# Idle products on TensorE in the tail of a convolution and attention kernel

## The reference

```
x = x + L0(_gn(x))     # _gn: group norm, 32 groups of 8 channels, per image
x = x + L1(_gn(x))
```

```
sim = jnp.where(mask, neg, sim)      # mask is true on real pixels
attn = jax.nn.softmax(sim, axis=-1)
out = jnp.einsum('bij,bjd->bid', attn, v)
out = out @ Wout_w.T + Wout_b
```

## Time and profile before

| | |
|---|---|
| device time of the three runs, median | 225.84 us |
| device time of the profiled execution | 225.6 us |
| its span, first to last instruction | 223.8 us |
| outside the span | 1.8 us |
| PE busy | 188.3 us (84% of the span) |
| DVE, ACT, POOL busy | 138.9, 134.8, 91.6 us |
| mean granted TensorE clock over the span | 0.98 |

### The profile page before, as it was taken

The page is one execution under the profiler, slowest core; times in us unless marked ns, Lnnn a source line. Parts: engine busy times, 40 slices in busy tenths (PEclk is TensorE's granted clock), DMA queues, the critical chain, the costliest instruction groups (busy, mean ns, idle before and its releaser), DMA issues.

```text
span 223.8 us, 3513 instructions
## 1 busy us (share of the span) xinstructions
PE 188.3 (84%) x1116; PEld 69.0 (31%) x1116; DVE 138.9 (62%) x338; ACT 134.8 (60%) x228; POOL 91.6 (41%) x203
## 2 busy tenths in 40 slices
PE   0003999799999999999999999999999999999440
PEld 0003243325323323233342333334333244334130
DVE  0487768956025866546665855867558675587932
ACT  0395779891324685909566595683955857559710
POOL 2005050524722513132396742359475139904331
PEclk9999999999999999999999999999999999999965
DMA  6999999995835769546867899799798898992705
GB/s 213 411 410 410 408 409 409 405 265 127 226 95 156 196 194 267 157 116 187 261 183 256 234 294 295 221 303 272 219 294 260 281 271 260 319 351 98 254 27 187
DMA packets 30802, 57.06 MB, mean 255 GB/s; under 512 B 3264, under 2 KB 12224, under 8 KB 30784
## 3 DMA queue, kind: packets, MB, share of 16 engines
q1 hardware_dynamic: 30400, 56.55, 78.8%
q10 hardware_dynamic: 384, 0.29, 0.4%
HBM read 17.85 MB, written 16.78 MB: 155 GB/s over the span
## 4 chain that ended last, share of the span: by engine, by line
PE 73%; DMA 9%; SPq 6%; DVE 4%; POOL 3%; ACT 2%; issue 1%; DVEq 0%; ACTq 0%; POOLq 0%
PE py L818 37%; PE pf L849 25%; DMA xs<-x_dram 9%; SPq L262 6%; PE pf L764 3%; PE py L866 3%; PE py L764 2%; DVE gs L560 2%; ACT junk L529 2%; POOL gs L353 1%; PE pf L778 1%; DVE xs L254 1%; POOL chain L400 0%; POOL chain L438 0%; POOL y L363 0%
## 5 line engine op out<-in xcount | busy, mean ns | idle before, releaser
L818 PE MATMUL py<-gs,wd 80*32 80x512 f32 x768 | 86.1, 594 | 0.0
L529 ACT ACTIVATE junk<-xs,nwb 128x1024 bf16<-128x1024 f32 x63 | 72.3, 1148 | 4.0 <-DVE xs L655 1.5
L655 DVE SCALAR_TENSOR_TENSOR xs<-pf,cst,xs 128x512 f32<-128x512 f32 x64 | 48.1, 751 | 21.0 <-PE pf L849 16.0
L849 PE MATMUL pf<-y,fw 128*128 128x512 f32 x128 | 59.1, 604 | 0.0
L509 ACT ACTIVATE y<-py,cst 128x512 f32<-128x512 f32 x32 | 20.3, 684 | 54.5 <-PE pf L849 49.6
L381 POOL TENSOR_TENSOR wd<-vals,cst 80x384 f32<-80x384 f32 x30 | 25.2, 844 | 56.2 <-PE py L818 55.9
L664 DVE SCALAR_TENSOR_TENSOR y<-py,cst,y 128x512 f32<-128x512 f32 x32 | 22.6, 747 | 35.1 <-PE py L818 35.0
L818 PEld LDWEIGHTS py<-gs,wd 80*32 80x32 f32 x768 | 23.1, 109 | 57.2 <-issue 56.5
L849 PEld LDWEIGHTS pf<-y,fw 128*128 128x128 f32 x128 | 23.0, 190 | 33.0 <-issue 33.0
L560 DVE BATCH_NORM_STATS2 gs<-xs 128x6 f32<-128x512 f32 x40 | 25.0, 681 | 12.0 <-DMA xs<-x_dram 11.9
L458 ACT ACTIVATE wd<-xs 128x1024 bf16<-128x1024 f32 x24 | 25.0, 1044 | 4.2 <-DMA xs<-x_dram 4.2
(11 more groups left out here) (84 smaller groups left out, 88.6 us busy)
## 6 DMA issues: line engine op xcount, KB each, us to landing
gs<-fc SPq DMA_DIRECT2D x128, 169.4 KB, 3.0
xs<-x_dram SPq DMA_DIRECT2D x15, 1024.0 KB, 18.8
out_dram<-xs SPq DMA_DIRECT2D x32, 256.0 KB, 3.1
out_dram<-xs SPq DMA_DIRECT2D x16, 512.0 KB, 3.9
xs<-x_dram SPq DMA_DIRECT2D x2, 512.0 KB, 17.3
gs<-wkv_dram SPq DMA_DIRECT2D x1, 256.0 KB, 15.5
gs<-wout_t_dram SPq DMA_DIRECT2D x1, 256.0 KB, 15.5
fw<-fusion_dram SPq DMA_DIRECT2D x1, 256.0 KB, 10.5
```

The source lines that it names most:

```text
L529: act.activation(junk[:, :], x1(n, c), func, scale=scale, bias=bias[:, c:c + 1], accum_out=acc[:, n, c, e:e + 1]).then_inc(s_stat, 1)
L655: dve.scalar_tensor_tensor(out=rows[:, t], in0=image(pf[:, bank * HALF:(bank + 1) * HALF]), scalar=fb[:, c:c + 1], in1=rows[:, t], op0=ALU ...
L818: mm = pe.matmul(py[n % 2][quad(q), s * HALF:(s + 1) * HALF], wd[0:KP, w0:w0 + QUAD], rows, start=(j == 0), stop=(j == PASSES - 1))
L849: pe.matmul(pf[:, bank * HALF:(bank + 1) * HALF], fw[:, t * C + 128 * c:t * C + 128 * (c + 1)], y[:, t * HALF:(t + 1) * HALF], start=True, ...
```

## The change

PE issues a product six times whose result nothing reads. Each is a float32 product of 128 x 512, of the shape of a fusion product, with its operands in place (`fw`, `y`) and its output in `py[0][:, 0:HALF]`, the bank that `attention(EARLY)` wrote. Four stand behind the last fusion and ahead of the last group product, two stand between the last group product and the last attention product. One wait is added ahead of the four: for `s_vec` at EARLY + 1, which DVE sets when it has copied the result of `attention(EARLY)` out of that bank. The products set no semaphore and wait for nothing else.

```diff
--- before
+++ after
@@ -911,8 +911,15 @@
                     f_late(3)
             pe.wait_ge(s_vec, EARLY)
             attention(EARLY)
+            def idle_products(count):
+                for _ in range(count):
+                    pe.matmul(py[0][:, 0:HALF], fw[:, 0:128], y[:, 0:HALF], start=True, stop=True)
+
             fuse(N - 1)
+            pe.wait_ge(s_vec, EARLY + 1)
+            idle_products(4)
             group_product(FINAL)
+            idle_products(2)
             attention(FINAL)
```

## The result

Over 20 executions of each kernel the changed one takes 225.31 us in the median (224.41 to 228.38), the kernel before 226.99 us (225.49 to 229.33). The ratio is 0.9948 with a 95% interval of 0.9926 to 0.9970: about 0.5% less, 1.2 us, and within the 1% that was called no change. The profiled execution takes 224.59 us at a span of 222.7 us (before: 225.6 and 223.8). Without that the means of the 20 give 0.9961 and the two medians 0.9926; why the medians jump is shown further down.

What follows compares the result with a forecast made beforehand. The prediction took the tail's chain of waits, with PE mostly idle and its clock falling before the last attention product, as the bound. Terms 0 + 0 + 0 + 0 - 0.85 us took 225.84 to 225.0 us, range 224.4 to 226.3.

Steps and rivals of the forecast that it cites:

- The term of the clock: Last attention product: clock stays at 1.00, so it takes 1.03 in place of 1.88 us, saving 0.85 us.
- The cost of the products: Idle products around the last group product: 0.43 us a record, hidden in PE's idle time, cost 0.
- The added wait: Behind the last fusion: the early result's copy is done some 3 us before PE waits for it, cost 0.
- DVE and ACT beside a busy PE: Tail residuals and statistics: not slowed by the idle products, bounded at 0 to 0.05 us, taken as 0.
- The reach to the end: Behind the last attention product: copy, adds and last stores follow it, so the whole 0.85 us reaches the end.
- The weight loads: Last attention product: eight loads follow the clock, 0.97 us high and 1.78 us low, against the skill's clock-independent rule.
- The rival of the overrun: Between last group and attention products: two idle products at low clock overrun their cover, 1.4 us late, 227.2 us; chance 0.05.
- The base of the sum: Whole kernel: level before taken as 225.84 us, the median of the runs, from which 0.85 us was subtracted.

Runs made afterwards that it cites:

- only the first fills: Kernel before plus four idle products (256, 512, 256, 384 columns) in PE's first-stage gaps, with nothing added in the tail; ratio 0.9970 (0.9940 to 0.9999).
- the pair alone: Changed kernel without the four products ahead of the last group product, keeping the two behind it; ratio to the kernel before 1.0013 (0.9980 to 1.0045).
- the second set: The unaltered changed kernel run once more against the kernel before, 12 executions; median 226.23 us, ratio 0.9948 (0.9910 to 0.9986).
- four and four: Changed kernel with four instead of two products between the last group and attention products; ratio to the kernel before 1.0003 (0.9966 to 1.0040).
- four only: Changed kernel without the two products behind the last group product, run twice; ratios to the kernel before 0.9956 first, 0.9970 second.

## Why the prediction was right

- *The time.* 225.0 us was forecast and 225.31 us measured, in the stated range of 224.4 to 226.3. Within 1% was right.
- *The term of the clock.* 0.85 us was forecast from the two attention products of before. The profile has 0.82 (1.88 to 1.06) for the product and 0.83 for the chain up to its end. Group by group over all executions (89 and 32), the mean span of the lowest group goes from 223.87 to 222.83 us and that of the next from 225.45 to 224.41, 1.04 us each. The ratio says 1.2 us, with an interval of 0.7 to 1.7 us on 227. I had written that nothing in the rows could be shortened beyond 0.85, since the group product ran at 1.00. That step was too narrow: the run with only the first fills shows a fall ahead of the group product, 0.2 us more to save, and the mean clocks say that the clock was low for longer than in the first profile in 26 of the 37 lowest executions of before.
- *The cost of the products.* 0.43 us a record and ends 0.4 and 0.2 us ahead of what follows were forecast; the distance is 0.43 (weight loads as before), the gaps left are 0.43 and 0.20 us. With two products more at either place the delay was 1.12 and 1.35 us, against an arithmetic of 1.1 to 1.3 and 1.3 to 1.5.
- *The added wait.* It cost nothing: the idle products begin at 209.10, 0.17 us ahead of the end of the fusion's last record (205.59 + 3.68), as a next record of the fusion would, since its records overlap by about as much (0.59 us long, 0.43 apart).
- *DVE and ACT beside a busy PE.* The tail's residuals stayed at 752 ns and the statistics at 1148 ns, as the rows said.
- *The reach to the end.* The last stores are issued from 218.2 (forecast 218.35), the span is 222.7 (forecast 222.95), 0.2 us of it from ahead of the tail.
- *The weight loads.* The rule of the page "TensorE: Matmul & The Clock Gate" of the Trainium skill, section "LDWEIGHTS (loading the stationary operand)", in which a load takes the same time at either clock, is not what these runs show: eight loads take 0.97 us in the changed kernel's tail, at 1.00, and 1.78 us at 0.50 in the kernel before. Since matrix instruction and load hang together in the rows, what is shown is that the whole product follows the clock.
- *The rival of the overrun.* Its mechanism is real, but not where I put the point of decision. I argued against it that the clock had been 1.00 up to 214.5 even without the four products. In the run with the pair alone the clock fell within the pair, and in that with the first fills alone at 213.1, ahead of the place where a pair would enter. That the pair costs nothing is the work of the four: with both, none of 32 spans lies between 223.2 and 224.1 or between 224.7 and 225.9, where a lost saving or the loss forecast here would put it.
- *The base of the sum.* This was the weakest step. I took the median of three, 225.84 us, as the level of the kernel before and 0.6 us as the scatter of a median. Twenty executions have 226.99, since over half lie in a group 1.5 us higher, and one of the three shown (227.42) was from it. From that level the same 0.85 us would have given 226.1. The forecast of 225.0 landed near 225.31 because 12 of the 20 executions of the changed kernel fell in the lower group; the second set had 3 of 12 there and a median of 226.23, still in the range, by 0.1 us. That the time came so close is luck; the term of the clock is not.

## What to carry to other kernels

Where a short product stands behind a wait on the path to the end, look at the granted clock in its window and at the same product elsewhere at the full clock; the difference is what keeping TensorE at work can win, here 0.82 us. Fill every gap behind the last dense stretch, not only the longest: with one of two gaps filled the gain came in half of the executions or not at all. A filling product is free only up to the releaser of what follows, and beyond it costs its full price at once, so leave a few tenths of a microsecond; and if executions fall into groups, compare the mean clock of each before explaining a median.

## What was not expected of the hardware

Gaps of about 1 us and less in the middle of a kernel were enough for a fall to 1.2 GHz in some executions and not in others, and their size doesn't decide: with 0.67, 0.95 and 0.48 us idle within 5 us the clock fell in one profile; with 1.16, 0.95 and 0.48 us at the same places it did not in the first profile of the changed kernel. The first of the three gaps, in the profile with four and four and in that of the changed kernel:

```profile
38.06 0.40 PE L748 MATMUL pf<-mv,cst 128*128 128x16 f32 x2 [0.67 <-DVE mv L581]
```

```profile
37.87 0.40 PE L748 MATMUL pf<-mv,cst 128*128 128x16 f32 x2 [1.16 <-DVE mv L581]
```

A fall costs about 1.6 us where the products behind it stand on the chain. The moment of the fall in the tail differed too: counted from the start of the last fusion it came after 7.4 us (first fills only), 8.8 us (before), 9.0 us (pair only) and 9.7 and 12.1 us (four only, second and first run). The first two have the same program in the tail, and so have the last two. The prediction cited the Trainium skill, page "TensorE: Matmul & The Clock Gate", section "What's actually happening", for a moment that moves between runs; these two pairs of profiles agree, with 1.4 and 2.4 us between them. And the clock column can't be used ahead of its first change: it shows 1.00 near 22 us, where 16 records of map products take 5.0 to 6.6 us instead of 3.65.
